# Up products of a feed-forward layer: seven block products for eight, by Strassen's scheme

## The reference

```
h = h + attention(layernorm(h) , cond)                  # 16 groups of 64 nodes, 8 heads
u = layernorm(h) @ geglu_w[i] + geglu_b[i]              # 1024 x 512 times 512 x 4096
val, gate = split(u, 2)                                 # 2048 columns each
h = h + (val * gelu(gate)) @ ffo_w[i] + ffo_b[i]        # 1024 x 2048 times 2048 x 512
```

## Time and profile before

| | |
|---|---|
| median of three runs | 2514.92 us |
| the profiled execution | 2514.83 us |
| its span, first to last instruction | 2513.0 us |
| TensorE busy | 2460.7 us, 98% |
| VectorE busy | 1346.8 us, 54% |
| ScalarE busy | 1034.6 us, 41% |
| GpSimd busy | 586.0 us, 23% |

### The profile page before, as it was taken

The page is one execution under the profiler, slowest core; times in us unless marked ns, Lnnn a source line. Parts: engine busy times, 40 slices in busy tenths (PEclk is TensorE's granted clock), DMA queues, the critical chain, the costliest instruction groups (busy, mean ns, idle before and its releaser), DMA issues.

```text
span 2513.0 us, 35583 instructions
## 1 busy us (share of the span) xinstructions
PE 2460.7 (98%) x12527; PEld 2041.8 (81%) x12527; DVE 1346.8 (54%) x2674; ACT 1034.6 (41%) x2144; POOL 586.0 (23%) x465
## 2 busy tenths in 40 slices
PE   6889999999999999999999999999999999999999
PEld 5448888888888888888888888888888888888887
DVE  8896676622236677622236677622236677622236
ACT  8964344532224334532224434532223434632223
POOL 2000000054440000054430000154430000154431
PEclk8989999999999999999999999999999999999999
DMA  2021100121210100022120000021110001022121
GB/s 76 10 93 38 34 34 17 35 69 65 67 56 34 34 34 18 34 76 66 60 71 18 34 34 34 18 84 59 67 63 21 31 33 34 18 84 67 59 102 62
DMA packets 29748, 122.02 MB, mean 49 GB/s; under 512 B 3120, under 2 KB 3504, under 8 KB 25008
## 3 DMA queue, kind: packets, MB, share of 16 engines
q1 hardware_dynamic: 29616, 120.31, 13.9%
HBM read 116.10 MB, written 4.19 MB: 48 GB/s over the span
## 4 chain that ended last, share of the span: by engine, by line
PE 92%; DVE 5%; ACT 2%; issue 1%; POOL 0%; DVEq 0%; ACTq 0%; POOLq 0%
PE ps L1574 27%; PE ps L1575 27%; PE ps L1576 27%; PE ps L1815 2%; PE ps L1832 2%; PE ps L1834 2%; DVE oh_d L1177 1%; PE ps L1829 1%; PE ps L1696 1%; PE ps L1697 1%; ACT full L802 1%; PE ps L1630 1%; PE ps L1842 1%; PE ps L1856 1%; PE ps L1744 0%
## 5 line engine op out<-in xcount | busy, mean ns | idle before, releaser
L1574 PE MATMUL ps<-xT_hi,wg_hi 128*128 128x512 f32 (+1 forms) x1104 | 414.2, 375 | 1.9 <-DVE xT_lo L1474 1.9
L1575 PE MATMUL ps<-xT_lo,wg_hi 128*128 128x512 f32 (+1 forms) x1104 | 412.5, 374 | 0.0
L1576 PE MATMUL ps<-xT_hi,wg_lo 128*128 128x512 f32 (+1 forms) x1104 | 412.4, 374 | 0.0
L1518 DVE SCALAR_TENSOR_TENSOR ff<-ps,cols_sb,gel 128x512 f32<-128x512 f32 x128 | 96.0, 750 | 574.0 <-ACT gel L898 574.0
L898 ACT ACTIVATE gel<-ps,cols_sb 128x512 f32<-128x512 f32 x128 | 88.1, 689 | 629.9 <-PE ps L1576 629.8
L464 POOL TENSOR_SCALAR veps<-mv 128x1 f32<-128x1 f32 x65 | 14.9, 230 | 1059.9 <-DVE mv L971 1059.9
L1527 DVE TENSOR_TENSOR h<-h,ps 128x512 f32<-128x512 f32 x256 | 174.9, 686 | 136.7 <-PE ps L1576 136.7
L1574 PEld LDWEIGHTS ps<-xT_hi,wg_hi 128*128 128x128 f32 x1104 | 207.7, 188 | 39.4 <-DVE xT_lo L1474 2.7
L1576 PEld LDWEIGHTS ps<-xT_hi,wg_lo 128*128 128x128 f32 x1104 | 207.7, 188 | 36.9
L1575 PEld LDWEIGHTS ps<-xT_lo,wg_hi 128*128 128x128 f32 x1104 | 207.8, 188 | 36.7
L1574 PE MATMUL ps<-cond_hi,w_hi 128*128 128x512 f32 x512 | 203.6, 398 | 0.0
(11 more groups left out here) (270 smaller groups left out, 5224.9 us busy)
## 6 DMA issues: line engine op xcount, KB each, us to landing
stage<-in_pieces SPq DMA_DIRECT2D x138, 512.0 KB, 3.3
stage<-in_condT SPq DMA_DIRECT2D x33, 1024.0 KB, 4.8
x<-in_x SPq DMA_DIRECT2D x2, 1024.0 KB, 6.9
at_s<-at SPq DMA_DIRECT2D x1, 2048.0 KB, 6.2
at16b<-at_s SPq DMA_DIRECT2D x1, 2048.0 KB, 9.3
out<-h SPq DMA_DIRECT2D x8, 256.0 KB, 2.0
bias_row<-in_rows SPq DMA_DIRECT2D x6, 256.0 KB, 3.5
raw<-in_condT SPq DMA_DIRECT2D x1, 1024.0 KB, 4.7
```

Source lines behind the costliest of these rows:

```text
L1518: dve.scalar_tensor_tensor(ff[:, s % 2, :], ps[:, step_bank(j, a, s, 0), :], cols_sb[:, bass.ds(COL["geglu_b"] + 32 * l + 4 * j + 2 * a + ...
L1574: pe.matmul(bank, l_hi, r_hi, start=(first and i == 0), stop=False)
L1575: pe.matmul(bank, l_hi, r_lo, start=False, stop=False)
L1576: end = pe.matmul(bank, l_lo, r_hi, start=False, stop=(last and i == n - 1))
```

## The change

Groups 1 to 7 of every layer no longer compute their up products step by step. For each column half c of a group the weights form a 2 x 2 matrix of blocks (feature half by value or gate, each 256 x 128), the features a 2 x 2 matrix (node half by feature half, each 256 x 512). Winograd's form of Strassen's scheme computes the four result blocks with seven block products, each two feature blocks of 128 with three matmuls of 512 columns. Group 0 stays as it was.

- The sums T1 to T4 of feature blocks are made once a layer by VectorE, in place in `z3` (`t_sums`), and split by ScalarE (`t_high`) and VectorE (`t_low`) into `w_hi`/`w_lo` places of the attention weights and a part of `xT3`. `x3_high` writes `z3` in place of `full`.
- The sums S1 to S4 of weight blocks are made for every group and half by VectorE (`weight_sums`) from `stage` into `sums_s`, which lies over `oT_hi`, `oT_lo`. Their high parts come from ScalarE, low parts from GpSimd.
- A set of weights is loaded by four DMAs that pick the half's blocks out of two pieces, so every up piece is read once per half.
- The seven products go to four PSUM banks; VectorE and ScalarE take partial sums out between them (`p1_copy`, `set_first`, `set_last`).
- Down products use banks 0 to 3 or 4 to 7 by turns. Attention pieces 5 to 7 of the next layer are loaded only after the last set. The loops over groups are written out.

The core of the diff (in the new lines, `r` counts the pieces of a layer; `n` the sets):

```diff
@@ SyncE
+    DOWN_PIECE = [2, 6, 10, 14, 18, 22, 25, 28]
+    AHEAD_PIECE = [5, 9, 13, 17, 21, 29, 30, 31]
...
+                def load_set(q, c):
+                    r = set_piece(q, c)
+                    place = stage[:, r % 2, :].rearrange("p (b k n) -> p b k n", b=4, k=2)
+                    sp.wait_ge(w_ok, FIRST_PIECES + PIECES * l + r - 1)
+                    for v in range(2):
+                        part = pieces[bass.ds(FIRST_PIECES + PIECES * l + 4 * q - 1, 2)]...
+                        for row in range(2):
+                            sp.dma_start(place[:, (1 + row, 3 * row)[v]], part[:, row]).then_inc(set_in[c], 16)
+                for r in range(2):
+                    load_piece(r, r)
+                for q in range(MG):
+                    load_down(q)
+                    if q + 1 < MG:
+                        for c in range(2):
+                            load_set(q + 1, c)
+                    if q < 5:
+                        load_ahead(q)
...
-                sp.wait_ge(w_ok, FIRST_PIECES + PIECES * l + PIECES)
+                sp.wait_ge(w_ok, FIRST_PIECES + PIECES * l + DOWN_PIECE[MG - 1] + 1)
                 load_raw(0)
                 wait_apart(sp, c_lo, 2 * GROUPS * l + 2 * GROUPS + 2)
+                for m in range(5, MG):
+                    load_ahead(m)
+                sp.wait_ge(w_ok, FIRST_PIECES + PIECES * l + PIECES)
                 load_raw(1)
@@ GpSimd
+                def set_low(q, c):
+                    pool.wait_ge(a_hi_ok, SETS * l + 2 * (q - 1) + c + 1)
+                    pool.tensor_tensor(lo[:, 0:3, :], stage[:, r % 2, 256:1024]..., bits(hi[:, 0:3, :]), ALU.subtract)
+                    pool.wait_ge(w_hi_ok, FIRST_PIECES + PIECES * l + r + 1)
+                    pool.tensor_tensor(lo[:, 3:7, :], sums_s[:, :, :], bits(hi[:, 3:7, :]), ALU.subtract).then_inc(w_ok, 1)
...
+                down_low(0)
+                f_low(0, 0, 0, 0)
+                f_low(0, 1, 0, 1)
+                set_low(1, 0)
+                f_low(0, 2, 1, 0)
+                f_low(0, 3, 1, 1)
+                set_low(1, 1)
+                ahead_low(0)
+                for q in range(1, MG):
+                    down_low(q)
+                    f_low(q, 0, 1, 0)
+                    f_low(q, 1, 0, 0)
+                    if q + 1 < MG:
+                        set_low(q + 1, 0)
+                    f_low(q, 2, 1, 1)
+                    f_low(q, 3, 0, 1)
+                    if q + 1 < MG:
+                        set_low(q + 1, 1)
+                    if q < 5:
+                        ahead_low(q)
+                ahead_low(5)
                 wait_apart(pool, f_ok, 2 + 32 * l + 32)
                 zero_q()
+                ahead_low(6)
                 rsqrt(norm0 + 2 * NT)
+                ahead_low(7)
@@ ScalarE
+                x3_high(6); gelu(0); down_high(0); t_high(1, 0); t_high(3, 0); x3_high(7)
+                f_high(0, 0, 0, 0); t_high(2, 0); gelu(1); blocks_high(1, 0); f_high(0, 1, 0, 1)
+                for n in (1, 3, 2):
+                    t_high(n, 1)
+                sums_high(1, 0); gelu(2); f_high(0, 2, 1, 0); gelu(3); t4_high(); f_high(0, 3, 1, 1)
+                blocks_high(1, 1); p1_copy(1, 0); sums_high(1, 1); ahead_high(0)
+                for q in range(1, MG):
+                    if q > 1:
+                        p1_copy(q, 0)
+                    down_high(q); set_gelu(q, 0, 0); f_high(q, 0, 1, 0); set_gelu(q, 0, 1)
+                    p1_copy(q, 1); f_high(q, 1, 0, 0)
+                    if q + 1 < MG:
+                        blocks_high(q + 1, 0)
+                    set_gelu(q, 1, 0)
+                    if q + 1 < MG:
+                        sums_high(q + 1, 0)
+                    f_high(q, 2, 1, 1); set_gelu(q, 1, 1); f_high(q, 3, 0, 1)
+                    if q + 1 < MG:
+                        blocks_high(q + 1, 1); sums_high(q + 1, 1)
+                    if q < 5:
+                        ahead_high(q)
@@ VectorE
+                def weight_sums(q, c):
+                    a21, a11, a12, a22 = (stage[:, r % 2, 256 * m:256 * m + 256] for m in range(4))
+                    wait_apart(dve, set_in[c], 64 * ((MG - 1) * l + q))
+                    dve.wait_ge(w_ok, FIRST_PIECES + PIECES * l + before_it + 1)
+                    dve.tensor_tensor(s1, a21, a22, ALU.add).then_inc(s_ok, 1)
+                    dve.tensor_tensor(s3, a11, a21, ALU.subtract).then_inc(s_ok, 1)
+                    dve.tensor_tensor(s2, s1, a11, ALU.subtract).then_inc(s_ok, 1)
+                    dve.tensor_tensor(s4, a12, s2, ALU.subtract).then_inc(s_ok, 1)
+                def set_first(q, c):
...
+                def set_last(q, c):
+                    wait_apart(dve, block_mm, 7 * n + 6)
+                    dve.scalar_tensor_tensor(value, ps[:, z, :], value_bias(q, c), pre, ALU.add, ALU.add)
+                    dve.wait_ge(f_ok, e + 1)
+                    dve.wait_ge(gel_ok, e + 1)
+                    dve.tensor_tensor(ff[:, 0, :], value, gel[:, 0, :], ALU.mult).then_inc(ff_ok, 1)
+                    dve.wait_ge(block_mm, 7 * n + 7)
+                    dve.tensor_tensor(gel[:, 1, :], ps[:, v, :], pre, ALU.add).then_inc(sum_ok, 1)
+                    dve.scalar_tensor_tensor(ff[:, 1, :], ps[:, x, :], value_bias(q, c), gel[:, 1, :], ...)
...
+                mlp_step(0); t_sums(0, (2, 4)); t_low(1, 0); x3_low(NT - 1); t_low(3, 0); mlp_step(1)
+                t_sums(1, (1, 3, 2, 4)); t_low(2, 0); weight_sums(1, 0)
+                for n in (1, 3, 2):
+                    t_low(n, 1)
+                mlp_step(2); add_bias(NT - 1); mlp_step(3); t4_low()
+                set_first(1, 0); weight_sums(1, 1); set_last(1, 0)
+                for q in range(1, MG):
+                    if q > 1:
+                        set_first(q, 0); set_last(q, 0)
+                    set_first(q, 1)
+                    if q + 1 < MG:
+                        weight_sums(q + 1, 0)
+                    set_last(q, 1)
+                    add_down(q - 1, range(2))
+                    if q + 1 < MG:
+                        weight_sums(q + 1, 1)
+                    else:
+                        cond_low(...)
+                    add_down(q - 1, range(2, NT))
+                add_down(MG - 1, range(NT))
@@ TensorE
+                def set_product(q, c):
+                    pe.wait_ge(w_ok, FIRST_PIECES + PIECES * l + set_piece(q, c) + 1)
...
+                    block_product(x, A11, c, moving_x(11))
+                    block_product(y, S2, c, moving_t(2))
+                    block_product(z, S1, c, moving_t(1))
+                    block_product(v, S3, c, moving_t(3))
+                    pe.wait_ge(p1_ok, n + 1)
+                    block_product(x, A12, c, moving_x(21), first=False)
+                    pe.wait_ge(sum_ok, 5 * n + 2)
+                    block_product(z, S4, c, moving_x(22), first=False)
+                    pe.wait_ge(sum_ok, 5 * n + 3)
+                    block_product(v, A22, c, moving_t(4), first=False)
+                for q in range(1, MG):
+                    for c in range(2):
+                        set_product(q, c)
+                    down_product(q - 1)
+                down_product(MG - 1)
```

More of the change, by code:

```diff
@@ L402, in _, with load_piece @@
                 wait_apart(sp, c_lo, 2 * GROUPS * l + 2 * GROUPS)
[L403 to L408, removed]
+                def load_piece(r, at):
+                    sp.wait_ge(w_ok, FIRST_PIECES + PIECES * l + r - 1)
+                    sp.dma_start(stage[:, r % 2, :], pieces[FIRST_PIECES + PIECES * l + at])                      .then_inc(stage_in[r % 2], 16)
@@ L551, in weights_low, with f_low @@
[L551 to L562, removed]
+                def f_low(q, s, half, c):
+                    pool.wait_ge(f_hi_ok, 32 * l + 4 * q + s + 1)
+                    pool.tensor_tensor(f_lo[q % 2][:, c, half * HALF:(half + 1) * HALF], ff[:, s % 2, :],
+                                       bits(f_hi[q % 2][:, c, half * HALF:(half + 1) * HALF]),
+                                       ALU.subtract).then_inc(f_ok, 1)
@@ L891, in _ @@
                 o_high(GROUPS * l + GROUPS - 1)
[L893 to L901, removed]
@@ L903, in f_high, with gate_bias @@
-                def f_high(j, a, s):
-                    half, c = s // 2, s % 2
-                    act.wait_ge(ff_ok, 32 * l + 8 * j + 4 * a + s + 1)
-                    act.activation(f_hi[a][:, c, half * HALF:(half + 1) * HALF], ff[:, s % 2, :], ACT.Copy)\
-                        .then_inc(f_hi_ok, 1)
-                def mlp_step(j, a, s, weights=True):
-                    gelu(j, a, s, weights)
-                    f_high(j, a, s)
-                def mlp_group(j, a, last=False):
-                    for s in range(4):
-                        mlp_step(j, a, s, not (last and s >= 2))
+                def gate_bias(q, c):
+                    return cols_sb[:, bass.ds(COL["geglu_b"] + 32 * l + 16 + 2 * q + c, 1)]
```

(11 more changed lines are left out.)

335 lines of the change are left out of this document (244 added, 91 removed).

## The result

The changed kernel takes 2592.55 us (median of four runs, 2591.7 to 2595.42) against 2515.44 us for the kernel before (four runs): ratio 1.0308, 95% interval 1.0291 to 1.0326, slower. The forecast was 2514.6 with a range of 2465 to 2551; the result lies 41 us above the range. The profiled execution took 2592.8 us.

The account below looks back on a forecast made before the run. TensorE, busy 98% of the span, was taken to bound the kernel. Removed matmuls -76.2 us, steady groups +14, into the feed-forward part +56, out of a layer +6 gave 2514.6 us, range 2465 to 2551.

Parts of the forecast that it names:

- the tie: Steady groups: GpSimd's 1024-column low part (18.7) and VectorE's value-gate product (18.8) want the port; given to VectorE, stall 0.7 us.
- rival 3: GpSimd wins at 18.7; value times gate waits 2.1 us: 36 us more, 2551 us, chance 0.27.
- the clock: TensorE's granted clock: taken to stay full; a fall during new stalls was named as a sign of being wrong.
- tile 6, groups 2 to 6: Down tile 6 waits for the addition of h tile 2: 0.7 us a group, 14 in all.
- xT_lo of tile 7: Into group 0: sums and low parts precede x3_low(7) on VectorE; stall 3.4 us a layer, 0.5 without the port.
- set (1,0): Group 1's first set waits for its low weights: stall 3.3 us a layer, near 0 without the port.
- set (1,1): Group 1's second set waits for weight sums made after set_first(1,0): stall 2.0 us a layer, port or no port.
- p1 of set (1,1): Piece 6 loads late, delaying gelu and p1_copy; p1 is free at 7.8, wanted at 5.44: stall 2.4 us a layer.
- group 1, tile 6: The same late weight sums stop down tile 6 in group 1: stall 3.0 us a layer.
- start, all four layers: Stalls into the feed-forward part, groups 0 and 1: 14.1 us a layer, 56 in all; 20 without the port.
- q_product: Between layers: load_raw(1) leaves late, so q_product starts some 1.3 us late, three times, 4 us.
- rivals 1 and 2: Rival 1: port costs little, 2465 us, chance 0.14. Rival 2: half of it, 2480 or 2494 us, chance 0.22.

Follow-up runs that it names:

- the kernel without the reads: The changed kernel with GpSimd's low parts of f and of the weight sets replaced by writes of zeros that read nothing: 2484.26 us (one run).

## Why the forecast was wrong

The step that failed is "In the earlier trace rows GpSimd dispatched 0.06 us earlier and still was the one delayed (3.68 us for two operations of 1.30), so I give it to VectorE", with the stall of 0.7 us that hangs on it; GpSimd won all 20 ties, and the wait was 2.04 to 2.09. The steps had the arrivals right (GpSimd 18.7, product 18.8; the trace has 0.09 between them). The evidence for the tie was thinner than I read it. The 3.68 us hold one GpSimd operation of 2.43 and one of 1.29, and beside the second, which starts at 2460.34 + 3.68 - 1.29 = 2462.73, it was VectorE that waited:

```profile
2462.73 2.37 DVE L1199 SCALAR_TENSOR_TENSOR at_lo<-at16b,at_hi 128x1024 fp32r<-128x1024 int16 x1
```

That is 2.37 us for 1.22. So the trace of before had one such pair each way, both with another data type on VectorE's side (int16). Moved by 0.1 us, the tie of the changed kernel goes the other way and 70 us with it. The forecast's own bound for the lost tie, 2.5 us a group, was near the 2.08 measured: rival 3, in place and kind.

The second failure is a term left out. The forecast named the clock under what would make it wrong and priced it at nothing: the trace of before has only short waits in this part. It cost 51 us, and with it even the range's upper end, rival 3's 2551, was too low.

By the forecast's own steps, in us of TensorE's wait:

| step | forecast | measured (layers 0 to 3) |
|---|---|---|
| matmuls removed | 336, 76.2 us | 336 |
| tile 6, groups 2 to 6 | 0.7 (0 to 2.5) | 2.04 to 2.09; 0.58 with the tie turned |
| xT_lo of tile 7 | 3.4 | 3.4, of which 0.5 was there before |
| set (1,0) | 3.3 | 1.6, 2.9, 0.4, 0.4; 3.0 each by starts |
| set (1,1) | 2.0 | 1.8 four times |
| p1 of set (1,1) | 2.4 | 3.7, 2.1, 3.8, 3.8 |
| group 1, tile 6 | 3.0 | 1.1, 2.4, 1.1, 1.1 |
| start, all four layers | 56 | 43 in waits; 62 by starts, clock included |
| q_product | 4 in all | 5.5 in all |
| after layer 3 | 2 | 0 |
| clock | 0 | 51, some 15 of it at the start |

- **Start.** The places were right, and the sum nearly so. The view of waits gives 43 us for 56, but a half-clock stretch ahead of a wait slows TensorE and so shortens the wait. From the restart at tile 7 to the first matmul of set (1,0) every layer takes 11.5 us, 3.0 more than the 8.45 before, whether the wait is listed with 2.9 or 0.4. To the restart at tile 6 of group 1 it is 47.8, 49.3, 47.8 and 47.9 us, where the matmuls need 35.7 at full pitch; with 2.9 a layer for tile 7 that makes 62 us.
- **The p1 copy** waited 3.7 us for 2.4. The down piece landed at 542.2 as forecast, but in every layer the product behind it lost the port to that piece's low part and took 2.2 us for 0.69, 1.5 us that the forecast's steps do not have:

```profile
543.34 2.37 POOL L552 TENSOR_TENSOR wf_lo<-stage,wf_hi 128x1024 fp32r<-128x1024 f32 x1 [2.19 <-ACT wf_hi L907]
544.08 2.18 DVE L1752 TENSOR_TENSOR ff<-o_full,gel 128x512 f32<-128x512 f32 x1 [7.38 <-ACT gel L1051]
```

- **The port** behaves as read between operations that read SBUF: one instruction at a time, handed over 0.14 us early. That it was the port, and not waits for results, the kernel without the reads shows in its durations.
- **The end** cost nothing: from the last row of transpositions (2447.44 and 2525.28) to the end of the span both kernels take 65.6 us.
- **DMAs.** The four 128 KB DMAs of a set (2.6 us to land) hold up nothing in the steady groups, as forecast.
- **Rivals.** Rival 3 had 0.27; rivals 1 and 2, the port costing little or half, 0.36 together, against durations in the earlier trace rows that already showed the clash. These were too high.

## What to carry to other kernels

Where two engines share a port and a step-by-step sum brings them there within 0.1 us of each other, the outcome is not a term of the sum but a fork: price both, and remove the tie (here by leaving one operand in PSUM) before the change is judged. A new wait of TensorE of about 2 us is to be priced with its length and with a possible fall of the clock, here 1.6 us more in 12 of 28 and in 17 of 20 cases. Removed matmuls pay only if the sums that replace them do not queue behind another engine: an eighth less in the up products of seven groups was turned into a loss of 3% of the whole, and one operation per set, put out of the clash, took that loss away.

## What was not expected of the hardware

- One write of one column (0.1 us) on GpSimd, in front of each low part of the weight sums, made the kernel 70 us faster (2592.55 to 2522.34).
- Of 28 equal waits of 2.04 us, 12 were followed by the lower granted clock and 16 were not; of 28 waits of 1.45 us, none was.
- A stretch at half clock does not always lengthen the kernel by its own loss: ahead of a wait it shortened the wait (set (1,0): 2.9 us listed without one, 0.4 with one of 6.8 us, the same 11.5 us between the restarts).
- GpSimd's writes did not hinder VectorE's two-input operations: 0.69 us beside a running row of them, where GpSimd's subtraction made it 2.85.
